# Residual sums issued as adding transfers by GpSimd, and another order of the scatters, in an AdaLN and mixture-of-experts kernel

## The reference, cut to what matters

```python
# hidden = x: (16, 256, 256), 16 batches of 256 tokens of width 256
z = relu(einsum('bsh,bhk->bsk', hidden, down_w[ids]) + down_b[ids])
y = hidden + einsum('bsk,bkh->bsh', z, up_w[ids]) + up_b[ids]
c = (y - mean(y)) * rsqrt(var(y) + 1e-5) * ln_g[ids] + ln_b[ids]
p = softmax(c @ gate_w + gate_b)                  # 8 experts
values, experts = top_k(p, 2)                     # values normed to sum 1
shared = gelu(c @ sh_w1 + sh_b1) @ sh_w2 + sh_b2  # inner width 1024
moe = sum over the 2 chosen experts e of value_e * (gelu(c @ ew1[e] + eb1[e]) @ ew2[e] + eb2[e])
out = x + c + shared + moe
```

## Time and profile before

| | us |
|---|---|
| median of the runs | 625.84 |
| the profiled execution | 622.08 |
| its span | 620.2 |
| TensorE busy (matmuls) | 594.8 |
| VectorE busy | 501.6 |
| ScalarE busy | 385.4 |
| GpSimd busy | 413.3 |

### The profile page before, as it was taken

The page is one execution under the profiler, slowest core; times in us unless marked ns, Lnnn a source line. Parts: engine busy times, 40 slices in busy tenths (PEclk is TensorE's granted clock), DMA queues, the critical chain, the costliest instruction groups (busy, mean ns, idle before and its releaser), DMA issues.

```text
span 620.2 us, 16942 instructions
## 1 busy us (share of the span) xinstructions
PE 594.8 (96%) x5119; PEld 483.3 (78%) x5119; DVE 501.6 (81%) x1212; ACT 385.4 (62%) x660; POOL 413.3 (67%) x326
## 2 busy tenths in 40 slices
PE   7889979999999999999999999999999999999994
PEld 3556646667566678788888888888888899999883
DVE  4999848879977966898989898989897587887862
ACT  2686928758776845767676767676755455555541
POOL 4564587989885611477868686858697567666682
PEclk9999999999999999999999999999999999999998
DMA  8985656575244945667657656665644335343212
GB/s 285 322 220 150 159 161 183 161 235 115 78 138 153 328 114 171 144 113 149 116 127 133 147 127 127 132 136 128 94 53 72 60 61 66 58 67 64 44 21 32
DMA packets 116740, 81.31 MB, mean 131 GB/s; under 512 B 71090, under 2 KB 106162, under 8 KB 116658
## 3 DMA queue, kind: packets, MB, share of 16 engines
q1 hardware_dynamic: 100802, 60.64, 39.7%
q0 software_dynamic: 13296, 16.92, 15.2%
q10 hardware_dynamic: 2560, 2.69, 1.4%
HBM read 43.21 MB, written 24.42 MB: 109 GB/s over the span
## 4 chain that ended last, share of the span: by engine, by line
PE 68%; DVE 8%; POOL 8%; issue 8%; ACT 4%; DMA 2%; SPq 0%; POOLq 0%; ACTq 0%; DVEq 0%
PE Y L1527 30%; PE H L1501 29%; PE Y L1419 5%; POOL xs_rows L534 3%; PE H L1404 3%; POOL wreg L502 2%; POOL wreg L512 2%; DMA wreg<-in_vecs 1%; ACT hf L685 1%; DVE hl L1160 1%; POOL wreg L516 1%; ACT L685 1%; DVE wreg L808 1%; ACT wreg L623 1%; DVE wreg L949 1%
## 5 line engine op out<-in xcount | busy, mean ns | idle before, releaser
L755 ACT ACTIVATE hf<-H,prme 128x256 f32<-128x256 f32 (+1 forms) x312 | 149.2, 544 | 95.9 <-issue 80.5
L1501 PE MATMUL H<-xT,wreg 128*128 128x256 f16 (+1 forms) x1872 | 194.4, 263 | 0.2
L1527 PE MATMUL Y<-wreg,hh 128*128 x1136 | 188.3, 273 | 0.8 <-DVE hl L1255 0.8
L1501 PEld LDWEIGHTS H<-xT,wreg 128*128 x1872 | 169.0, 98 | 18.9 <-issue 1.0
L1527 PE MATMUL Y<-wreg,hl 128*128 x568 | 154.8, 273 | 0.0
L1527 PEld LDWEIGHTS Y<-wreg,hh 128*128 128x128 f16 x1136 | 111.1, 98 | 15.4 <-issue 1.5
L1255 DVE SCALAR_TENSOR_TENSOR hl<-hf,prme,hh 128x512 f16<-128x512 f32 (+1 forms) x156 | 115.8, 742 | 5.6
L1253 DVE TENSOR_SCALAR hh<-hf,prme 128x512 f16<-128x512 f32 (+1 forms) x156 | 91.1, 584 | 32.5 <-ACT hf L755 30.1
L588 POOL DMA_INDIRECT out_y<-hl,xgm x38 | 69.2, 1820 | 60.6 <-DVE hl L1282 40.9
L577 POOL TENSOR_SCALAR b2w<-b2t,wsel 128x256 f32<-128x256 f32 x71 | 97.9, 1602 | 15.1 <-DVE wsel L1270 9.6
L1404 PE MATMUL H<-xT,wreg 128*128 128x512 f16 x384 | 88.9, 379 | 6.8 <-ACT hf L685 4.7
(11 more groups left out here) (208 smaller groups left out, 663.6 us busy)
## 6 DMA issues: line engine op xcount, KB each, us to landing
stage<-in_w SPq DMA_DIRECT2D x16, 1024.0 KB, 6.2
b2t<-in_b SPq DMA_DIRECT2D x39, 128.0 KB, 3.3
wreg<-in_wpack SPq DMA_DIRECT2D x16, 256.5 KB, 4.7
wreg<-in_xt SPq DMA_DIRECT2D x16, 256.0 KB, 5.3
wreg<-in_vecs SPq DMA_DIRECT2D x16, 256.0 KB, 4.1
out_y<-wreg SPq DMA_DIRECT2D x16, 256.0 KB, 2.8
wreg<-in_x SPq DMA_DIRECT2D x14, 256.0 KB, 5.2
xs_rows<-wreg SPq DMA_DIRECT2D x9, 260.0 KB, 7.1
```

The costliest lines, as they stand in the source:

```text
L755: act.activation(hf[:, c, half * w:(half + 1) * w], H[c][:, half * w:(half + 1) * w], ACT.Gelu_apprx_tanh, bias=pr[:, ch:ch + 1], scale=pr ...
L1501: m = pe.matmul(H[c][:, half * w:(half + 1) * w], we[:, bass.ds(e + h * 2048 + k * 1024 + col, P)], xp[:, a + k, 0:w], start=i == 0, stop= ...
L1527: m = pe.matmul(result(n, j), hx[:, n % 2, c * w + j * P:c * w + (j + 1) * P], we[:, bass.ds(e + 4096 + h * 2048 + c * D, D)], start=c == ...
```

## The change

Two edits. The sums `x + c` are no longer additions on GpSimd: GpSimd issues for each batch one transfer from `yb` to `acc` (256 KB, within SBUF) with `accum_op` add. The sum is complete when the transfer's semaphore, one of four `d_acc`, has risen by 16; the waits on `q_acc` become waits on these. The second edit is in the order of GpSimd's scatters: pair 0's four blocks stand in the slots 5, 5, 5, 6 and no longer 5, 6, 7, 7 (12, 12, 12, 13 after its base), its blocks 0 and 3 still ahead of the slot's other work, its blocks 1 and 2 and all of pair 1's now behind `rows`, `xb`, `residual` and `tokens`.

```diff
--- before.py
+++ after.py
@@ -88,6 +88,8 @@
 
 def block_slot(p, i):
 
+    if p == 0:
+        return 12 + i // 3
     if p < PT or p == NP - 3:
         return 12 + min(i, 2)
     return 11 + i if p < NP - 2 else 10 + (p < NP - 1) + i // 2
@@ -292,7 +294,8 @@
         ve_lo, v_yo, v_sel = (sem("v_" + n) for n in ("elo", "yo", "sel"))
 
         q_set, q_ident, q_tri, q_iota = (sem("q_" + n) for n in ("set", "ident", "tri", "iota"))
-        q_xb, q_xn, q_acc, q_tok, q_b2 = (sem("q_" + n) for n in ("xb", "xn", "acc", "tok", "b2"))
+        q_xb, q_xn, q_tok, q_b2 = (sem("q_" + n) for n in ("xb", "xn", "tok", "b2"))
+        d_acc = [sem(f"d_acc{i}") for i in range(4)]
         q_root, v_var, v_first, v_w1, v_part, q_const = (sem(n) for n in ("q_root", "v_var", "v_first", "v_w1", "v_part", "q_const"))
         out_rows = out.rearrange("b s d -> (b s) d")
 
@@ -302,6 +305,10 @@
                 eng.wait_ge(v_first, b + 1)
             else:
                 eng.wait_ge(q_xn, b - 1)
+
+        def summed(eng, b):
+
+            eng.wait_ge(d_acc[b % 4], 16 * (b // 4 + 1))
 
         def scattered(eng):
 
@@ -493,7 +500,7 @@
                 pool.wait_ge(d_up[b % 3], 16 * (b // 3 + 1))
                 pool.wait_ge(d_x[b % 12], 16 * (b // 12 + 1))
                 if b >= 4:
-                    pool.wait_ge(q_acc, b - 3)
+                    summed(pool, b - 4)
                 if b >= 4 + 2 * PT:
                     pool.wait_ge(v_xl, b // 2 - 1 - PT)
                     pool.wait_ge(a_xh, b // 2 - 1 - PT)
@@ -513,7 +520,7 @@
 
             def residual(b):
                 normed(pool, b)
-                pool.tensor_tensor(acc_of(b), acc_of(b), yb_of(b).rearrange("p (j d) -> p j d", j=2), ALU.add).then_inc(q_acc, 1)
+                pool.dma_start(acc_of(b), yb_of(b).rearrange("p (j d) -> p j d", j=2), accum_op=ALU.add).then_inc(d_acc[b % 4], 16)
 
             def tokens(p):
                 if p >= 3:
@@ -548,10 +555,9 @@
             for s in range(NS):
                 for p in at(s, 3):
                     root(p)
-                for p in range(PT):
-                    for i in range(4):
-                        if s == base(p) + block_slot(p, i):
-                            scatter(p, i)
+                for i in (0, 3):
+                    if s == base(0) + block_slot(0, i):
+                        scatter(0, i)
                 for p in at(s, 5):
                     rows(2 * p)
                     rows(2 * p + 1)
@@ -563,9 +569,9 @@
                     residual(2 * p)
                     residual(2 * p + 1)
                     tokens(p)
-                for p in range(PT, NP):
+                for p in range(NP):
                     for i in range(4):
-                        if s == base(p) + block_slot(p, i):
+                        if s == base(p) + block_slot(p, i) and (p, i) not in ((0, 0), (0, 3)):
                             scatter(p, i)
 
             def weigh_bias(n):
@@ -644,7 +650,8 @@
                 rank, m = UNITS[u]
                 if m == 0 and rank == 2:
                     act.wait_ge(v_xl, NP - PT)
-                    act.wait_ge(q_acc, B)
+                    for b in range(B - 4, B):
+                        summed(act, b)
                     act.wait_ge(p_up, B)
                     act.wait_ge(v_etab, 1)
                     act.wait_ge(d_pad, 16 * (NE + 1))
@@ -1163,7 +1170,7 @@
             def shared_rows(b):
                 pr = prm[:, NE, :]
                 dve.wait_ge(p_y, b + 1)
-                dve.wait_ge(q_acc, b + 1)
+                summed(dve, b)
                 a = acc_of(b).rearrange("p j d -> p (j d)")
                 dve.scalar_tensor_tensor(a, Y[b % 2][:, :], pr[:, 10:11], a, ALU.mult, ALU.add).then_inc(v_acc, 1)
```

## The result

The changed kernel took 619.79 us, median of 10 runs (616.82 to 622.59), the kernel before 624.58 us beside it (10 runs, 623.42 to 626.19). The ratio is 0.9923, 95% interval 0.9901 to 0.9944: 4.8 us faster. The forecast was 621.0 us in a range of 617.5 to 628.0. The profiled execution took 617.43 us, its span is 615.4 us.

A forecast was written before the change was run, and what follows sets the result against it. TensorE was taken to bound the kernel, with only its idle time in the first 230 us to win. Gains of 4.0 and 1.3 less 0.5 us made 4.8 us, so a median of 621.0 us, range 617.5 to 628.0.

The forecast's parts named there:

- The bound: Expert stage after 230 us is TensorE's own work; only TensorE's idle time in the first 230 us can be won.
- Part 1, the scatter order: Scatters moved behind the shifts of batches 6 and 7 remove TensorE stalls of 3.50 and 0.52 us: 4.0 us gained.
- Part 2, the issue: Issuing a sum as a transfer costs GpSimd 1.9 us, up to 1.2 us more per pair than additions.
- Rival A: Dear issues, 3.6 us each, delay GpSimd in slots 9 to 20: 7 us slower, 633; deciding from about 2.7; chance 0.13.
- Part 2, the landing: Sums land in 4.5 us, bounds 2.5 and 9.0; `xb(8)` starts at 80.2 or 82.1 us; `xb(4)`'s wait costs 0.
- Rival B: Sum 4 lands late, 7 us after the issue's end; TensorE still waits 1.4 us: gain 2.7, 623.1 us; chance 0.15.
- The Trainium skill's rule: A GpSimd-issued transfer takes about 2.0 us plus its bytes over 436 GB/s: estimate 2.6 us for 256 KB.
- Part 3, VectorE: VectorE freed from GpSimd's additions shortens TensorE's waits at 160.55 and 183.33 us: 1.3 us gained, bounds 0 and 2.0.
- The losses: Scatters at 64 to 69 us share engines with pair 2's transposes, and sums add traffic: 0.5 us, bounds 0 and 1.5.
- my signs of being wrong: Sum issues above 2.7 us, `xb(8)` waiting past 84, new TensorE idle between 100 and 190, first pair's shift after 38.
- Rival C: GpSimd and VectorE set the pace from 100 to 186 us; only up to 1 us is left: 625; chance 0.15.
- The sum: 4.0 + 1.3 - 0.5 = 4.8 us less: span 615.4 us, median 621.0 us; forecast's chance 0.46.

The follow-up runs named there:

- experiment 5: Changed kernel with one idle GpSimd power operation behind each whole residual transfer, adding GpSimd time and no packets: 631.37 us, ratio 1.0076 to the kernel before.
- the halves: Changed kernel with each residual sum issued as two transfers of half the size, 32 issues in all: 624.22 us, ratio 0.9988 to the kernel before.
- the partners: The two kernels with the sums of pairs 3 to 7 left in slot 6: changed kernel unedited, 621.64 us; with added zero products, 621.16 us.
- experiment 12: Changed kernel with sums of pairs 3 to 7 issued in slot 5 and more zero products at TensorE's start: 618.99 us, ratio 0.9913 to the kernel before.
- 11: Changed kernel with 24 instead of 20 zero products at TensorE's start and 5 more behind the first U product: 621.16 us, ratio 0.9935 to the kernel before.
- experiment 1: Kernel before with the new scatter order alone, residual sums still additions on GpSimd: 622.97 us, ratio 0.9969 to the kernel before.
- experiment 9: Changed kernel with nothing edited, measured again on another chip: 621.64 us, ratio 0.9934 to the kernel before.

## Why the prediction was right, step by step

**The bound.** Right: the expert stage is untouched (0.06 us idle in 440 to 600), and the gain came before it. From the first shared product to the first expert product it is 198.3 us before (25.06 to 223.4) and 192.3 after (25.46 to 217.8), 6.0 us less. A start 0.4 us later and an expert stage 0.8 us longer, with one new wait (0.51 us at 249; the 0.78 us at 251 has its like in 0.77 at 256.69 before), leave 4.8 of the span.

**Part 1, the scatter order.** The mechanism is right: shifts end at 84.66 (forecast 84.0 to 85.9), both stalls are gone, ScalarE's wait is 3.88 us (3 to 6). The 3.50 and 0.52 us are gone with the order alone as well. What that kernel measured was 2.0 us and not 4.0, since it pays elsewhere: 0.8 us more at pair 2's transposes, 0.99 us at 96.50 behind an addition that slows VectorE, and perhaps the 2.2 us behind slot 28, which may be the chip's.

**Part 2, the issue.** Wrong by a factor of two in size: 1.9 us forecast for one sum, 0.94 us measured, under even my lower bound of 1.26 us, because no gap of 0.3 us stands ahead of these issues, as it does ahead of a scatter; the bare 0.94 us is what a scatter takes (0.96). The step drawn from it, that a dearer issue costs nothing, is wrong as well. At 2.2 us a sum (the powers) the kernel is 4.8 us slower than before, or 2 to 3 if the stretch behind slot 28 is the chip's, where Rival A put the deciding point at 2.7. At 1.83 us (the halves) 2 to 4 us of the gain is given back, in part perhaps for the packets. So had the issue been as dear as I forecast, a part of the gain, at worst nearly all of it, would have been lost: the error in the size hid the error in the step. Rival A's premise of 256 runs of 1 KB is out: the packets of GpSimd's queue rose from 13296 to 15600, 144 a transfer, and its bytes from 16.92 to 21.12 MB.

**Part 2, the landing.** 4.5 us forecast, 6.7 us median measured (3.9 to 8.4, inside the bounds). A part of that comes from issuing two at once: with a power between them (experiment 5) the same transfers land in 4.6 us median (3.9 to 5.8). `xb(8)` began at 80.95, in the forecast's 80.2 to 82.1, only because the issue came 0.9 us sooner. Rival B's mechanism was there but its price wasn't: the wait of 4.09 us reached nobody, as TensorE's full stretches from 80 to 100 us show. `xb(4)` waited 1.01 us in the first profile and began at 33.24, before the allowed 34.9: cost 0, right. The Trainium skill's rule (DMA: Bandwidth & Descriptors, "Anatomy of one DMA"), by which an estimate of 2.6 us was given, doesn't hold for this transfer: the shortest of 16 took 3.9 us. (Counted from the issue's end the estimate puts the landing at 75.65 + 1.9 + 2.6 = 80.2, not before 80 as the forecast says; nothing hangs on it.)

**Part 3, VectorE.** Right, and larger: both stalls of VectorE's (1.34 and 0.64 us) are gone, 2.0 us instead of 1.3. The forecast that no row of the low half near the sums exceeds 2.5 us holds near the sums alone; 2.60 us (at 107.66) stand beside a shift, 2.54 (118.70) and 3.03 (143.70) beside an `xb`, which are additions on GpSimd too.

**The losses.** 0.5 us forecast for the scatters at pair 2's transposes and the added traffic. The loss at pair 2 is there, though the first profile hides it: 0.52 us in it, but 1.67 in the second of the same kernel, 1.34 with the order alone and 1.25 without any sum, against 0.51 and 0.48 in the two profiles with the old order. So it goes with the scatters' place and not with the sums, as forecast, and at 0.7 to 1.2 us in these three it is more than the 0.5 that I took for all losses. A second loss I didn't place: the routing waits 1.08 us in the first profile and 3.05 us in the second for transposes that land late, and new TensorE idle time between 100 and 190 was among my signs of being wrong. In the run without sums TensorE had no wait of 0.1 us or more from 95 to 200 us, so in that comparison it is the sums that make these waits. Issuing those of pairs 3 to 7 one slot ahead leaves 0.35 and 0.58 us of them, where the partners had 3.05 and 3.30. Why the move helps is open. That it keeps the transfers away from the transposes would fit, but the transposes' median landing is no shorter for it (4.9 us in experiment 12, 4.3 in 11; longest 6.5 against 7.3), and the move changes the order of GpSimd's other work as well.

**Rival C (given back)** didn't come true as a whole: 150:160 is now full. But it named the place that is nearly full, and the delay added to GpSimd by the powers was paid there.

**The sum.** 4.8 us forecast and 4.8 us measured. The terms were 4.0 + 1.3 - 0.5. In the first profile 6.0 us of stalls went, 1.1 us came at the routing, some 1.1 us less was waited elsewhere, and 1.2 us went to the later start and the expert stage: 4.8. In the second the routing alone has 2 us more. The ratios of the edits alone, 2.0 and 0 us, can't be held against the terms because of the stretch behind slot 28. That the removed stalls are those forecast is no luck; that the total agrees to 0.1 us is, and so is the span (615.4): the changed kernel's executions spread over 5.8 us.

## What to carry to other kernels

Follow a wait back to what the engine did meanwhile, and move what nobody waits for: here six scatters stood ahead of two shifts, and 3.50 us went with them. Cost each edit on the path that the others leave: with the additions still there, the new order laid them beside VectorE's line 954 (4.17 us for 1.28). When an engine is 80 to 90% busy in the stage, its time isn't free: 1.25 us more for each of 16 sums cost 7 to 9.6 us, while a wait of 4 us for a landing at one place reached nobody. The slot in which bulk transfers are issued is worth a try of its own: one slot earlier brought 1.3 to 2.4 us for pairs 3 to 7, and at pair 2 a wait of 3.94 us. And when experiments don't run beside the result, compare a stretch that no edit touches before you compare sizes.

## What the hardware showed that I had not expected

- An adding transfer of 256 KB within SBUF costs GpSimd 0.94 us, and 1.83 us in two halves: in this pair of runs it goes by the number of transfers, not by bytes. It lands 3.9 to 8.4 us later (median 6.7) when two are issued at once, longer than the loads of the same size from HBM in the profile (5.1 us for x), and 3.9 to 5.8 us later (median 4.6) with 1 us between the two.
- GpSimd's issues leave VectorE alone (1.28 us for two of line 956 beside them), its additions don't (3.56 us before; 4.29 us for a single one in experiment 1).
- TensorE's granted clock fell to 0.50, the level of 1.2 GHz, between 15 and 20 us in some executions and not in others. What TensorE did before doesn't tell them apart: in experiment 9 it was busy 4.84 of the 5 us from 5 to 10 and the clock fell, in the profile of before 4.61 and it stayed at 1.00. In the two profiles with nine more products it stayed at 1.00 too, and the kernel was no faster for it.
